# Six row buffers in place of three for the expert tiles of a routed transformer layer, loaded five tiles ahead

## The reference, cut to what matters

```python
def reference(...):
    x = L0_attn_inputs
    x = _layernorm(x + attention_and_dense_ffn(x))
    # the experts
    logits = einsum('btd,ed->bte', x, router_w)
    mask = one_hot(argmax(softmax(logits)), E)
    h = square(relu(einsum('btd,edh->ebth', x, expert_fc)))
    out_e = einsum('ebth,edh->ebtd', h, expert_proj)
    return _layernorm(x + einsum('ebtd,bte->btd', out_e, mask))
```

## Time and profile before

| | us |
|---|---|
| median of 3 runs | 921.11 |
| lowest and highest | 919.39, 926.2 |
| the profiled execution | 927.96 |
| its span | 926.0 |
| PE busy (7164 matmuls) | 813.7 |
| DVE busy | 578.2 |
| ACT busy | 311.3 |
| POOL busy | 328.3 |

### The profile page before, as it was taken

One profiled execution on the slowest core, in us unless ns is written; L12 is line 12 of the kernel. 1 busy time (PEld: TensorE's weight loads), 2 busy tenths in 40 slices (PEclk: granted clock), 3 DMA queues, 4 the chain that ended last, 5 costly groups with the idle time before them and its releaser, 6 DMA issues.

```text
span 926.0 us, 19416 instructions
## 1 busy us (share of the span) xinstructions
PE 813.7 (88%) x7164; PEld 602.1 (65%) x7164; DVE 578.2 (62%) x1340; ACT 311.3 (34%) x571; POOL 328.3 (35%) x433
## 2 busy tenths in 40 slices
PE   7879899999999999999989998996977876887695
PEld 3457676776776776776767777885654644655553
DVE  7978787988888888889888475552322312322222
ACT  2423224435335344344342343112221321332232
POOL 8110431417336246146164364521321321331333
PEclk9979999999999999999998999998988977988988
DMA  8999992101001010000004094658556546646730
GB/s 263 281 293 303 304 288 70 43 2 47 25 2 64 7 40 31 2 25 24 1 24 178 1 301 139 211 172 340 185 225 250 191 177 245 218 155 248 256 115 11
DMA packets 75197, 133.27 MB, mean 144 GB/s; under 512 B 5726, under 2 KB 54112, under 8 KB 75105
## 3 DMA queue, kind: packets, MB, share of 16 engines
q1 hardware_dynamic: 71936, 123.57, 41.0%
q0 software_dynamic: 3168, 8.46, 2.5%
HBM read 89.35 MB, written 42.93 MB: 143 GB/s over the span
## 4 chain that ended last, share of the span: by engine, by line
PE 71%; DMA 10%; DVE 7%; SPq 4%; issue 4%; ACT 2%; POOL 1%; POOLq 0%; ACTq 0%; DVEq 0%
DMA xs<-routed_rows 10%; PE bank L981 7%; PE bank L833 6%; PE bank L865 6%; PE bank L845 6%; PE bank L876 5%; PE bank L993 5%; PE bank L643 5%; PE bank L795 4%; PE bank L759 4%; PE bank L811 4%; PE bank L961 3%; PE bank L946 3%; PE bank L652 2%; PE bank L787 2%
## 5 line engine op out<-in xcount | busy, mean ns | idle before, releaser
L1296 POOL TENSOR_TENSOR rstd<-vare,minus_half 128x1 f32<-128x1 f32 x96 | 54.0, 565 | 272.8 <-DVE vare L1574 272.5
L1769 DVE COPY token<-xs 128x1 int32<-128x1 int32 x34 | 5.2, 154 | 161.3 <-PE bank L993 87.8
L946 PE MATMUL bank<-xsT,fc 128*128 128x128 f32 x800 | 95.9, 279 | 2.4 <-DVE act L1755 1.7
L946 PEld LDWEIGHTS bank<-xsT,fc 128*128 128x128 f32 x800 | 93.3, 195 | 5.8 <-issue 5.5
L1351 POOL TENSOR_TENSOR mrstd<-mvare,minus_half 128x1 f32<-128x1 f32 x34 | 19.3, 566 | 207.6 <-DVE mvare L1776 207.6
L1565 DVE TENSOR_TENSOR sm<-bank,upto 128x512 f32<-128x512 f32 x128 | 79.4, 683 | 19.9 <-PE bank L759 19.9
L981 PE MATMUL bank<-pj,act 128*128 x336 | 77.4, 383 | 4.5 <-issue 4.0
L1157 ACT ACTIVATE relu<-bank 128x512 f32<-128x512 f32 x68 | 40.1, 595 | 96.6 <-PE bank L946 63.6
L981 PEld LDWEIGHTS bank<-pj,act 128*128 128x128 f32 x336 | 62.1, 190 | 14.8 <-issue 6.7
L833 PE MATMUL bank<-n1T,w1s 128*128 128x256 f32 x256 | 68.2, 389 | 2.9 <-ACT hT L1106 2.4
L865 PE MATMUL bank<-n1T,w1s 128*128 128x256 f32 x256 | 69.3, 395 | 1.3 <-ACT hT L1123 0.8
(11 more groups left out here) (267 smaller groups left out, 1693.8 us busy)
## 6 DMA issues: line engine op xcount, KB each, us to landing
routed_rows<-empty SPq DMA_DIRECT2D x64, 520.0 KB, 9.7
fc<-in_fc SPq DMA_DIRECT2D x31, 1024.0 KB, 6.4
up_unit<-in_fc SPq DMA_DIRECT2D x24, 1024.0 KB, 8.3
pj<-in_pj SPq DMA_DIRECT2D x8, 1024.0 KB, 11.8
xrow<-in_fc SPq DMA_DIRECT2D x6, 1024.0 KB, 7.3
x<-in_x SPq DMA_DIRECT2D x8, 512.0 KB, 3.7
xT<-in_xT SPq DMA_DIRECT2D x7, 512.0 KB, 5.1
xs<-routed_rows SPq DMA_DIRECT2D x25, 130.0 KB, 2.3
```

Source lines behind the costliest of these rows:

```text
L946: last = nc.tensor.matmul(h_bank[n][:, chunk(f)], fc[:, at, k, chunk(4 * n + f)], xsT[:, k, :], start=(k == 0), stop=(k == KT - 1))
L1296: nc.gpsimd.tensor_tensor(rstd[:, n, c], vare[:, n, c], minus_half[:], ALU.pow)\
```

## The change

`xs` gets six buffers (`ROWS`), each with its semaphore. `load_rows(j)` waits for `res` of tile j-6. Rows 3 to 5 are loaded right behind rows 0 to 2; in the early part the rows of tile j+3 are issued after the weights of tile j; at the seam SP issues the rows of tiles 9 and 10 before the up weights of tile 10, and the rows of tile 11 before the first unit weights; in the loop iteration j issues the weights and then the rows of tile j+5 in place of j+2. The eight semaphores `gone[g]` become two, one for the groups 0 to 3 and one for 4 to 7, and each waiter waits for all 32 clearing DMAs of its half. A few small SBUF tiles are shared (`count_i` for `early_i` and `begin_i`, `unit_expert` for `tile_at_i`, `begin_late` for `begin_units`, `room` for `units_room`), and the unused rooms grow.

```diff
+GPG = G // 2
+ROWS = 6
 def rows_in(j):
-    return sum(16 * (UPT if of_units(n) else 1) for n in range(j % 3, j + 1, 3))
+    return sum(16 * (UPT if of_units(n) else 1) for n in range(j % ROWS, j + 1, ROWS))
-EARLY_ROOM, DOWN_ROOM = 512, 2784
+EARLY_ROOM, DOWN_ROOM = 904, 3170
-        xs = s2("xs", [P, 3, ROW])
+        xs = s2("xs", [P, ROWS, ROW])
-        scattered, gone = [sem("scattered0"), sem("scattered1")], [sem(f"gone{g}") for g in range(G)]
+        scattered, gone = [sem("scattered0"), sem("scattered1")], [sem("gone0"), sem("gone1")]
-        xs_in = [sem(f"xs_in{n}") for n in range(3)]
+        xs_in = [sem(f"xs_in{n}") for n in range(ROWS)]
...
-                        .then_inc(gone[g], 16)
+                        .then_inc(gone[g // GPG], 16)
...
-                M["res"].wait(sp, j - 3, 1)
+                M["res"].wait(sp, j - ROWS, 1)
...
-            for g in range(G):
-                sp.wait_ge(gone[g], 16 * E)
+            for part in range(2):
+                sp.wait_ge(gone[part], 16 * E * GPG)
...
             for j in range(3):
                 load_rows(j)
                 load_up(j)
+            for j in range(3, ROWS):
+                load_rows(j)
...
             for j in range(3, EARLY):
                 load_up(j)
-                load_rows(j)
+                if ROWS <= j + 3 < EARLY:
+                    load_rows(j + 3)
             sp.wait_ge(rt, R_EXPERT)
             load_up(EARLY)
-            load_up(EARLY + 1)
             sp.wait_ge(rt, R_DONE)
...
             load_rows(EARLY)
+            load_rows(EARLY + 1)
+            load_up(EARLY + 1)
             sp.wait_ge(rt, R_UNITS)
+            load_rows(EARLY + 2)
             for n in range(RING - 1):
                 load_unit_up(n)
-            load_rows(EARLY + 1)
+            load_rows(EARLY + 3)
             load_unit_up(RING - 1)
-            load_rows(EARLY + 2)
+            load_rows(EARLY + 4)
             for j in range(EARLY, SLOTS):
...
-                if EARLY + 3 <= j + 2 < SLOTS:
-                    load_rows(j + 2)
+                if j + 5 < SLOTS:
+                    load_rows(j + 5)
...
-                pool.wait_ge(gone[g], E * 16)
+                pool.wait_ge(gone[g // GPG], 16 * E * GPG)
```

More of the change, by code:

```diff
@@ L276, in build @@
         acc, begin_at = sb("acc", [P, E]), sb("begin_at", [P, E])
-        begin_i = sb("begin_i", [P, E], I32)
         minus_half = sb("minus_half", [P, 1])
@@ L280, in build @@
         parity = sb("parity", [P, 2])
-        early, early_i = sb("early", [P, E]), sb("early_i", [P, E], I32)
-        tile_at, tile_at_i = sb("tile_at", [P, UNITS]), sb("tile_at_i", [P, UNITS], I32)
+        early = sb("early", [P, E])
+        tile_at = sb("tile_at", [P, UNITS])
         count_i, filled = sb("count_i", [P, E], I32), sb("filled", [P, E])
@@ L288, in build @@
         expert, at_tile = sb("expert", [P, FULL], I32), sb("at_tile", [P, FULL], I32)
-        took, begin_units, units_room = sb("took", [P, E]), sb("begin_units", [P, E]), sb("units_room", [P, E])
+        took = sb("took", [P, E])
         unit_expert, at_unit = sb("unit_expert", [P, UNITS], I32), sb("at_unit", [P, UNITS], I32)
@@ L550, in load_rows @@
                     if of_units(j) else [of_tile(at_tile, full_of(j), E * NT)]
-                M["res"].wait(sp, j - 3, 1)
+                M["res"].wait(sp, j - ROWS, 1)
                 if of_units(j):
                     for u in range(UPT):
-                        sp.dma_start(xs[u * UNIT:(u + 1) * UNIT, j % 3],
+                        sp.dma_start(xs[u * UNIT:(u + 1) * UNIT, j % ROWS],
                                      units_d[:, bass.ds(places[u], 1), :].rearrange("p a r -> p (a r)"))\
-                            .then_inc(xs_in[j % 3], 16)
+                            .then_inc(xs_in[j % ROWS], 16)
                 else:
-                    sp.dma_start(xs[:, j % 3], tiles_d[:, bass.ds(places[0], 1), :].rearrange("p a r -> p (a r)"))\
-                        .then_inc(xs_in[j % 3], 16)
+                    sp.dma_start(xs[:, j % ROWS], tiles_d[:, bass.ds(places[0], 1), :].rearrange("p a r -> p (a r)"))\
+                        .then_inc(xs_in[j % ROWS], 16)
             units_d = xs_d.rearrange("(s p) r -> p s r", p=UNIT)
@@ L923, in turn_rows @@
                     ev["sm"].wait(pe, G - 1, 4 * NC)
-                pe.wait_ge(xs_in[j % 3], rows_in(j))
+                pe.wait_ge(xs_in[j % ROWS], rows_in(j))
                 M["xsT"].wait(pe, j - 1, 1)
                 for m in range(KT):
-                    last = nc.tensor.transpose(x_bank[:, chunk(m)], xs[:, j % 3, chunk(m)], ident[:])
+                    last = nc.tensor.transpose(x_bank[:, chunk(m)], xs[:, j % ROWS, chunk(m)], ident[:])
                 last.then_inc(M["turned"].sem, 1)
@@ L1262, in _ @@
             make(nc.gpsimd.memset(pair_sum[:], 0.0))
[L1263 to L1269, removed]
+            make(nc.gpsimd.iota(count_i[:], [[1, E]], base=-E, channel_multiplier=0))
+            make(nc.gpsimd.tensor_copy(early[:], count_i[:]))
+            make(nc.gpsimd.iota(count_i[:], [[NT * P, E]], base=0, channel_multiplier=0))
+            make(nc.gpsimd.tensor_copy(begin_at[:], count_i[:]))
+            make(nc.gpsimd.tensor_copy(acc[:], count_i[:]))
+            make(nc.gpsimd.iota(unit_expert[:], [[1, UNITS]], base=0, channel_multiplier=0))
+            make(nc.gpsimd.tensor_copy(tile_at[:], unit_expert[:]))
             pool.sem_inc(masks_done, 1)
@@ L1733, in units_left @@
                 step(nc.vector.tensor_tensor(taken[:], taken[:], took[:], ALU.add))
-                step(nc.vector.scalar_tensor_tensor(begin_units[:], taken[:], float(P), begin_at[:], ALU.mult, ALU.add))
-                step(nc.vector.tensor_tensor(filled[:], acc[:], begin_units[:], ALU.subtract))
+                step(nc.vector.scalar_tensor_tensor(begin_late[:], taken[:], float(P), begin_at[:], ALU.mult, ALU.add))
+                step(nc.vector.tensor_tensor(filled[:], acc[:], begin_late[:], ALU.subtract))
                 step(nc.vector.tensor_scalar(count_i[:], filled[:], float(UNIT - 1), None, ALU.add))
@@ L1739, in units_left @@
                 step(nc.vector.tensor_scalar(taken[:], taken[:], float(UPT), None, ALU.mult))
-                step(nc.vector.tensor_scalar(units_room[:], taken[:], -1.0, float(NT * UPT), ALU.mult, ALU.add))
-                step(nc.vector.tensor_tensor(units_room[:, 0:E - 1], units_room[:, 0:E - 1], taken[:, 1:E], ALU.add))
+                step(nc.vector.tensor_scalar(room[:], taken[:], -1.0, float(NT * UPT), ALU.mult, ALU.add))
+                step(nc.vector.tensor_tensor(room[:, 0:E - 1], room[:, 0:E - 1], taken[:, 1:E], ALU.add))
                 step(nc.vector.tensor_scalar(late_at[:], tile_at[:], taken[:, 0:1], None, ALU.add))
-                tiles(filled, lambda out: nc.vector.tensor_tensor(out, units_room[:], filled[:], ALU.subtract),
+                tiles(filled, lambda out: nc.vector.tensor_tensor(out, room[:], filled[:], ALU.subtract),
                       late_at[:], unit_expert[:], at_unit[:], UNITS, E * NT * UPT)
@@ L1765, in finish @@
                 M["down"].wait(dve, j, 1)
-                dve.wait_ge(xs_in[s], rows_in(j))
+                dve.wait_ge(xs_in[j % ROWS], rows_in(j))
                 if j >= 3:
                     dve.wait_ge(y_out[s], j // 3 * 16)
-                nc.vector.tensor_copy(token[:, s:s + 1], xs[:, s, D:D + 1].bitcast(I32)).then_inc(M["token"].sem, 1)
-                nc.vector.tensor_tensor(res[:, s], made_in[:, 0:D], xs[:, s, 0:D], ALU.add).then_inc(M["res"].sem, 1)
+                nc.vector.tensor_copy(token[:, s:s + 1], xs[:, j % ROWS, D:D + 1].bitcast(I32)).then_inc(M["token"].sem, 1)
+                nc.vector.tensor_tensor(res[:, s], made_in[:, 0:D], xs[:, j % ROWS, 0:D], ALU.add).then_inc(M["res"].sem, 1)
                 M["res"].wait(dve, j, 1)
```

## The result

The changed kernel takes 837.02 us (median of 4 runs, 833.92 to 839.23), the kernel before 920.25 (4 runs, 918.85 to 926.2); the ratio is 0.9072, with a 95% interval of 0.9025 to 0.9119. The direction, the place and the cause came out as forecast; the size was too small.

The account below looks back on a forecast made before the run. The prediction took PE's waits for late rows queued behind weight loads as the bound: 75.5 us from waits and slow matmuls, less 3.8 for the clock, gives 71.7 off the 921.11 median, so 849 us, range 840 to 867.

Parts of the forecast that it names:

- 3.8 us taken off for the clock: Loop before the tail: clock stays at 0.98, not its upper level, costing 2% of 190 us.
- The 14 waits go: Experts' part: all 14 PE waits for rows vanish with rows five tiles ahead, 57.7 us.
- Seven slow `down_mixed`: Loop: seven `down_mixed` behind long waits fall from 5.67 to 3.65 us each, 14.1 us.
- The slow transposes and the slow `down` at the seam: Eight transposes behind waits go from 0.69 to 0.44 us, 2.0 us; the seam's `down` from 5.43 to 3.69, 1.7 us.
- rival B: Loop: small waits of 0.4 us keep the mean clock at 0.90, 17 us more, 866; chance 0.08.
- The prediction's terms for tile 10: Seam: tile 10's 7.70 us wait, its slow transposes (0.69 to 0.44) and slow `down` (5.43 to 3.69) go.
- What is late next: Loop at a 24.3 us period: weights, POOL and ACT's copies stay in time, so PE alone is the bound.
- The 7 us of idle DMA per period: Loop: 7.1 MB at 414 GB/s takes 17.2 of 24.3 us, leaving 7 us of DMA idle.
- Rival A: Loop: weights become the bound in part; at 270 GB/s a period takes 26.3 us, 864; chance 0.09.
- Rivals C and D: C: waits for rows stay, 921, chance 0.04; D: denser demand slows loads, `up_mixed` waits for units, 932, chance 0.03.
- The seam, the early part, the two clearing semaphores: Seam and early loads: 0, bounds -1 and +4 us; clearing semaphores: nothing waited for, over 80 us of cover.

Follow-up runs that it names:

- old_seam: Changed kernel with the seam's issue order of before (tile 10's up weights ahead of tile 9's rows, tile 10's rows behind five unit loads): 846.71 us.
- before_own_early: Kernel before, with PE reading the expert number of down(j-1) ahead of its wait for rows: 916.95 us against 921.57.
- more_8mb: Changed kernel plus four 1 MB DRAM copies behind the unit loads of each of the first seven mixed tiles: 884.84 us.
- eight_gone: Changed kernel with a clearing semaphore for each of the eight groups again: 837.06 us.
- four_buffers: Changed kernel with four row buffers, rows three tiles ahead instead of five, and no rows of tiles 12 and 13 at the seam: 855.08 us.
- three_rows_first: Kernel before with its three buffers, rows of tile j+2 issued ahead of the weights in each loop iteration: 913.71 us.
- late_full: Changed kernel with full tiles' rows from tile 15 on two tiles ahead again, place number read behind the added wait: 880.53 us.

## Why the prediction was right in kind and too small

The step that failed is the price of a wait: the sum took each wait at its listed idle time, with a slow clock behind the long ones alone, and put the gap before `down` behind the short ones at nothing. That came to some 7 us. A second term, 3.8 us taken off for the clock, should not have been there. The lower end of the range, 840, had room for either but not for both. Term by term:

*The 14 waits go* (57.7 us): right, none is left.

*Seven slow `down_mixed`* (14.1 us): right. The group fell from 39.7 us to 25.6, which is 14.1.

*The slow transposes and the slow `down` at the seam* (2.0 and 1.7 us): right in kind. The prediction's terms for tile 10 came to 7.7 + 0.25 + 1.7 = 9.65; between the `up`s of tiles 9 and 10 the trace of before took 17.65 us against 7.32 after, 10.3 more. That `old_seam` gives back 9.7 us is no finer check, given its interval.

*"It won't quite: the densest long stretch of this trace has 0.98. ... 3.8 us"*: wrong. Each period after has a clock of 1.00. The 0.98 of the first 450 us is unchanged by the change, and was no measure for a stretch in which PE doesn't pause. I took a mean of one kind of work for a property of another.

*What the small waits cost.* This is the larger term that was mis-sized. The prediction counted a short wait at the idle time that the list puts to it, and used the 0.41 us "issue" gap before `down` only as a point for rival B, as if it were there in any case. But the gap is part of the wait: PE reads the expert's number in its program behind the wait for rows, and after the change it has read it long before. The second full `up` of a period started in before's timeline of PE at

```profile
753.10 3.84 PE L946 MATMUL bank<-xsT,fc 128*128 128x128 f32 x32
```

and from there to the transposes behind `up_mixed` it took 765.16 - 753.10 = 12.06 us with a wait of 0.15, against 692.28 - 681.27 = 11.01 after. So this short wait cost 0.9 us beyond its own length. The six stretches of this kind in before, with waits of 0.13 to 0.82 us, all show the same 0.9 us; the wait of tile 11 at the seam shows 1.4. Over the seven that is 6.8 us beyond the idle time counted. With the read moved ahead (`before_own_early`) the same stretch takes 11.41 us with a wait of 0.15, and all six show 0.25 us beyond the wait: some 0.65 of the 0.9 us was the register read, and 0.25 is left of the restart. Between medians that move recovers 4.6 us.

So in the profiled executions, from the `up` of tile 9 to the end, before took 926.0 - 633.5 = 292.5 us and after 834.7 - 627.9 = 206.8: 85.7 us gained, against 71.7 forecast. Of the 14 missing, 3.8 are the clock's term, 6.8 the short waits, about 2 lie around the long waits (1.5 over the seven of the loop, 0.6 at the seam, not tried by themselves), and the rest is spread over small differences. The part ahead of tile 9's `up` was 5.6 us shorter after, but that says nothing of the change: the traces that share the changed kernel's code there reach this `up` anywhere from 626.9 to 632.5 us. Between medians the gain is 83.2 us; the profiled execution of before was slower than all of its timed runs.

*What is late next.* "PE is then the bound by itself" was right, and no engine or transfer took the waits' place. The 7 us of idle DMA per period were 4 to 5: the sustained rate in `more_8mb` is 384 GB/s, not the 414 of a two-microsecond stretch, and the period is shorter.

*Rival A* did not happen, and the added traffic shows where it would. *Rival B* did not happen: the small gaps went with the waits, and the clock stayed up. The Trainium skill ("TensorE: Matmul & The Clock Gate", section "A second HAM failure mode: psum-queue depth-cycling") warns of clock swings from short idle times; the loop after, at 1.00 in each period, doesn't show them. Short waits can be followed by the lower clock in this program, though. At 566.8 us in the trace of before, in the early tiles, behind two waits of 1.3 and 0.9 us, an `up` took 5.41 us where it takes 3.74:

```profile
564.92 0.44 PE L892 MATMUL bank<-ident,xrow 128*128 128x128 f32 x2 [1.34 <-ACT xrow L1130]
566.26 0.41 PE L927 MATMUL bank<-ident,xs 128*128 128x128 f32 x2 [0.90 <-ACT xsT L1147]
...
566.78 5.41 PE L946 MATMUL bank<-xsT,fc 128*128 128x128 f32 x32
```

The trace of after has the same two waits, and the `up` behind them at full pace:

```profile
562.17 0.44 PE L898 MATMUL bank<-ident,xrow 128*128 128x128 f32 x2 [1.45 <-ACT xrow L1136]
563.52 0.41 PE L933 MATMUL bank<-ident,xs 128*128 128x128 f32 x2 [0.92 <-ACT xsT L1153]
...
564.04 3.74 PE L952 MATMUL bank<-xsT,fc 128*128 128x128 f32 x32
```

Of the fourteen traces ten have this `up` slow and four don't, so that one trace alone doesn't tell what such a wait costs. Whether this is the swing that the Trainium skill describes isn't shown; where PE is kept full, there is none. *Rivals C and D* did not happen.

*The seam, the early part, the two clearing semaphores*: forecast at 0, and `eight_gone` shows 837.06 for the last. The seam's order was not nothing, though. The prediction had its gain inside the 14 waits and only looked for a loss there; `old_seam` shows that rows issued ahead of the unit loads are what saves tile 10, and `four_buffers` shows the same for tile 12, mixed there with later unit loads. Tile 11's short wait, 1.27 us before, is in neither.

*Why five tiles and not one fewer wait.* What the prediction never asked was whether the waits are independent. They aren't, and this is a lesson beside the forecast, not a part of its error, since the change moves all rows at once. With both kinds of rows late the kernel takes 904.7, with only the full tiles' late 880.5 (in an edit that reads the number late), with only the mixed tiles' late 882.2, with none 837.0. Making one kind early gains 22 to 24 us, making both gains 68. Where one wait goes, the next rows meet a fuller queue and a PE that comes earlier, as `three_rows_first` shows in its plainest form.

## What to carry to other kernels

A small transfer issued behind large ones on one queue needs a distance that covers the large ones' time, for every reader of that queue: repairing the worst wait alone moves it to the next small transfer. When pricing a wait, add what comes behind it: the slow clock (here behind every wait of 2.8 us and more, and behind some of 1.9 to 2.75 us) and the register reads that stand behind it in program order. Take the time between two fixed points with and without it rather than the idle time listed. Put register reads ahead of waits; on PE it was worth 4.6 us here, on SP 26 us where all rows were late and less than 5 us where half of them were. A deeper buffer also frees the issuing engine: with four buffers SP stood at one row load, and the weights behind it left 7.6 us later.

## What was not expected of the hardware

The same wait was followed by the higher or the lower clock from one execution to the next. From 590 us on, in the fourteen traces together, every wait of PE of 2.8 us and more had slow matmuls behind it (the next block of 16 to 64 took 4.7 to 6.5 us against 3.5 to 3.7), of the seven waits from 2.3 to 2.75 us three had, and no single wait under 1.85 us had. The wait for `act` ahead of the `up` of tile 7 is in thirteen of the traces, at 1.7 to 1.9 us; behind it the `up` runs at full pace in ten and takes 5.44 us in three. One of the three is `late_full`, whose granted clock is 0.50 from 618 to 620 us:

```profile
615.58 5.44 PE L955 MATMUL bank<-xsT,fc 128*128 128x128 f32 x32 [1.86 <-DVE act L1764]
```

What decides between the two is not shown.

With the queue never empty, DMA moved 381 to 387 GB/s over the stretches of 30 us shown above, 7% under the 408 to 414 of 2 us stretches behind weight loads. The changed kernel, without any copies, moved 399 GB/s from 627.9 to 642.6 us. How the kind of transfer and the length of the stretch share in this was not tried.
